# A state-space scan over 32 batches: where in TensorE's step the sum of a past state stands

## What is computed

```python
dA = jnp.exp(jnp.einsum('bld,dn->bldn', dt, A))          # 512 channels, 16 states
dB = jnp.einsum('bld,bln->bldn', dt, Bm)
def step(h, inp):
    dA_i, dB_i, u_i, C_i = inp
    h = dA_i * h + dB_i * u_i[:, :, None]
    y = jnp.einsum('bdn,bn->bd', h, C_i)
    return (h, y)
...
out = y * jax.nn.silu(z)
return out @ W_out.T
```

## Time and profile before

| | us |
|---|---|
| median of 2 runs | 3286.52 |
| lowest, highest | 3284.66, 3288.39 |
| the profiled execution, its time | 3282.21 |
| the profiled execution, its span | 3280.3 |
| granted TensorE clock, mean over the span | 0.967 |

### The profile page before, as it was taken

How to read it: one execution, slowest core, us unless ns; L and a number is a source line. 1 busy time by engine, 2 the same in 40 slices (tenths; PEclk the granted TensorE clock), 3 DMA queues, 4 the chain that set the end, 5 groups by cost and what they waited for, 6 DMA issues and landing times. The chain is left out here.

```text
span 3280.3 us, 54538 instructions
## 1 busy us (share of the span) xinstructions
PE 2964.9 (90%) x19138; PEld 2406.4 (73%) x19138; DVE 2839.4 (87%) x4799; ACT 2710.2 (83%) x5234; POOL 2229.4 (68%) x911
## 2 busy tenths in 40 slices
PE   6999999999999999999999999999999997566664
PEld 4777787777777777777787878787887877455453
DVE  4889999999999999999999999999999998544442
ACT  5999999999999999999999999999999996211110
POOL 1777676666766666666767676767767676377776
PEclk8999999999999999999999999999999999688888
DMA  3112211222222222211222222212222111477774
GB/s 112 59 59 69 70 59 61 68 71 70 71 70 62 65 70 71 71 61 60 69 70 71 71 70 70 71 61 70 71 70 71 61 56 33 129 148 148 149 150 78
DMA packets 196175, 252.98 MB, mean 77 GB/s; under 512 B 45664, under 2 KB 174144, under 8 KB 195904
## 3 DMA queue, kind: packets, MB, share of 16 engines
q1 hardware_dynamic: 171328, 211.73, 20.6%
q0 software_dynamic: 24576, 37.77, 7.0%
HBM read 188.36 MB, written 61.08 MB: 76 GB/s over the span
## 5 line engine op out<-in xcount | busy, mean ns | idle before, releaser
L354 POOL TENSOR_TENSOR hid<-hid,c_all 128x1536 f32<-128x1536 f32 x512 | 1770.1, 3461 | 873.9 <-DVEq L617 872.4
L622 DVE TENSOR_TENSOR_SCAN hid<-decay,hid,psB 128x1024 f32<-128x1024 f32 x512 | 1201.5, 2347 | 76.9 <-PE psB L942 27.6
L397 ACT ACTIVATE decay<-dt,a_neg 128x383 f32<-128x383 f32 x2048 | 1085.3, 604 | 0.0
L942 PE MATMUL psB<-ident,dbu_t 128*128 128x128 f32 x5760 | 806.0, 276 | 82.4 <-DVE hid L622 67.6
L385 ACT ACTIVATE dbu_t<-dtu_t,b_t 128x512 f32<-128x512 f32 x1312 | 853.2, 714 | 17.7 <-PE psB L942 16.6
L942 PEld LDWEIGHTS psB<-ident,dbu_t 128*128 128x128 f32 x5760 | 657.6, 142 | 245.3 <-issue 113.5
L954 PE MATMUL psY<-ident,hid 128*128 128x128 f32 x6144 | 758.0, 273 | 1.0 <-POOL hid L354 1.0
L954 PEld LDWEIGHTS psY<-ident,hid 128*128 128x128 f32 x6144 | 690.7, 142 | 1.6 <-POOL hid L354 1.3
L622 DVE TENSOR_TENSOR_SCAN hid<-decay,psB 128x512 f32<-128x512 f32 x512 | 623.0, 1217 | 10.3 <-PE psB L942 6.3
L1024 PE MATMUL psM<-u,w_dt 128*128 128x384 f32 x1024 | 349.1, 489 | 4.8 <-ACT u L427 3.3
L1422 ACT ACTIVATE e_sg<-e_psU 128x256 f32<-128x256 f32 x64 | 24.5, 383 | 340.3 <-PE e_psU L1464 225.4
(11 more groups left out here) (156 smaller groups left out, 3570.1 us busy)
## 6 DMA issues: line engine op xcount, KB each, us to landing
c_all<-bc_rows_dram SPq DMA_DIRECT2D x128, 768.0 KB, 4.9
out_dram<-h SPq DMA_DIRECT2D x64, 384.0 KB, 3.0
h<-out_dram SPq DMA_DIRECT2D x32, 384.0 KB, 3.6
x_weights_dram<-normed SPq DMA_DIRECT2D x32, 384.0 KB, 2.6
xt<-in_x_t_dram SPq DMA_DIRECT2D x32, 375.0 KB
xs<-in_x_dram SPq DMA_DIRECT2D x32, 256.0 KB
e_wg<-in_gate_dram SPq DMA_DIRECT2D x64, 128.0 KB
e_wu<-in_up_dram SPq DMA_DIRECT2D x64, 128.0 KB
```

Source lines behind the costliest of these rows:

```text
L354: nc.gpsimd.tensor_tensor(hid[k % 4][:, :, :], hid[k % 4][:, :, :], c_all[:, k, :].unsqueeze(1).to_broadcast([P, CH, L]), ALU.mult).then_i ...
L397: last = nc.scalar.activation(decay[k % 4][:, c, 1:L], dt[q][:, c, 1:L], ACT.Exp, scale=a_neg[:, c, k:k + 1])
L622: nc.vector.tensor_tensor_scan(h[:, lo:hi], flat(decay[k % 4])[:, lo:hi], flat(psB)[:, lo:hi], h[:, lo - 1:lo] if j else 0.0, ALU.mult, AL ...
L942: last = nc.tensor.transpose(flat(psB)[:, i * P:(i + 1) * P], dbu_t[k % 2][:, t, c * P:(c + 1) * P], ident[:, :])
```

## The change

In TensorE's loop the two calls of `sum_y` move from between the two groups of turns to behind the second. What stood between the groups otherwise (k=2 and k=5) stays there, and all that stood behind group 1 now stands behind group 1 and the sum. Nothing else is changed: no instruction, no wait, no buffer, no DMA, and no other engine's program.

```diff
@@ -1082,10 +1082,6 @@
                 for k in range(NS):
                     if scans:
                         turn_dbu(b, q, k, 0)
-                    if scans and k >= 3:
-                        sum_y(b, k - 3)
-                    if back and k < 3:
-                        sum_y(m, k + NS - 3)
                     if k == 2:
                         if front:
                             project_xin(n, 0)
@@ -1096,6 +1092,10 @@
                             route(c)
                     if scans:
                         turn_dbu(b, q, k, 1)
+                    if scans and k >= 3:
+                        sum_y(b, k - 3)
+                    if back and k < 3:
+                        sum_y(m, k + NS - 3)
                     if k == 0:
                         if front:
                             turn_normed1(n, 0)
```

## The result

The changed kernel takes 3495.49 us (median of 2 runs, 3493.82 to 3497.16) against 3286.52: a ratio of 1.064, 95% interval 1.062 to 1.066. It is 209 us slower, where 153 had been forecast; the time lies within the range, close to its upper end. The profiled execution took 3497.16 us with a span of 3495.3, to be set beside 3280.3.

A forecast was written before the change was run, and what follows sets the result against it. VectorE was taken to set the pace, with TensorE following closely. Terms 79.1 + 33.0 + 26.0 + 9.6 + 21.1 - 15.5 = 153 us, added to the kernel before, gave 3440 us, range 3395 to 3500.

The forecast's parts named there:

- the walk: One batch followed from the places where TensorE waited for VectorE: 153 us slower, own range 3410 to 3470, chance 0.60.
- rival 1: TensorE's clock falls at step 3 after new idle: 43 to 69 us more if in every batch, 3483 to 3509; chance 0.18.
- gate: At k=2 VectorE waits for TensorE's sum of state 15 before gating batch m's output: 2.55 us, 31 batches.
- row maximum: At k=5 VectorE waits for the scores, a 16.78 us TensorE path after step 3's idle: 1.10 us, 30 batches.
- short scan of step 8: VectorE's scan waits for TensorE, counted from step 5's long scan: 0.84 us in 31 batches.
- short scan of step 11: VectorE's scan waits for TensorE, counted from step 9's long scan: 0.32 us in 30 batches.
- out block and what leads to it: At k=15 VectorE waits to add the out block, counted from step 13's long scan: 0.68 us, 31 batches.
- given back at the long scans: VectorE's earlier waits for TensorE's turns vanish, as group 1 comes no later: 0.5 us a batch, 15.5 us.
- the two consequences: Sum no longer fills TensorE's wait before group 1, later work up to 1.31 us late; next group 0 1.31 us late.
- rival 2: ScalarE's lead over the scans is used up and its 1.3 us wait is paid too: up to 3480, chance 0.08.
- The time with only the gate paid: Only VectorE's wait at the gate is paid, the other four terms could vanish: 3350 us, chance 0.10.
- The case of no slowdown: VectorE's 0.5 us a batch is given back and nothing is paid: 3271 us, chance 0.04.

The follow-up runs named there:

- step 2 alone: Kernel before, with the sum moved behind both groups of turns in step 2 only: 3328.2 us, ratio 1.014.
- all but step 3: Changed kernel with the sum of step 3 put back between the groups: 3427.3 us, ratio 1.044.
- steps 8 and 15 alone: Kernel before, with the sum moved behind both groups in steps 8 and 15 only: 3273.1 us, ratio 0.9974.
- the filled step 3: Changed kernel with group 0's four turns in step 3 made four times in all batches but the first: 3467.8 us, ratio 1.057.
- The filled runs: Two runs: changed kernel with group 0's turns in step 3 made four times (3467.8 us) or twice (3478.6 us).

## Why the prediction was right, and where it fell short

The direction, the mechanism and the places were right. The number was 56 us too low: 3495 lies above the 3410 to 3470 that the walk had for its own range, and it is within the stated range because that one was drawn to hold rival 1. The clock of rival 1 makes 30 of the 56, the other 26 are terms that came out larger than forecast; that both together still fit under 3500 is luck.

Term by term, for a batch at the full clock (1537.51 to 1628.56), us a batch:

| term | forecast | measured shift |
|---|---|---|
| gate | 2.55 | 2.69 |
| score of the experts | 0 | 0.46 |
| row maximum | 1.10 | 1.28 |
| short scan of step 8 | 0.84 | 0.84 |
| short scan of step 11 | 0.32 | 0.32 |
| out block and what leads to it | 0.68 | 0.72 |
| given back at the long scans | -0.50 | -0.35 |
| sum | 4.99 | 5.96 |

Gate to gate it is 91.05 - 84.98 = 6.07; the remaining 0.11 are shifts under 0.06 each.

**The bound and the two consequences** were right. VectorE set the pace; each of its new waits was paid in full, and the waits stand at the five places named, ended by the releasers named. The run with step 2 alone bears it out: with one sum on its path the gate waits 1.31 us, with two 2.62. One wait that VectorE pays at the full clock, that of the score, had not been named.

**The missed term** is the score, 0.46 us, and it belongs to the sum for row maximum. The sum of 16.78 us counted TensorE's z projection of step 5 at its issue price, as if its buffer were free. It isn't:

```profile
1553.64 1.98 PE L1014 MATMUL psM<-w_in,turned 128*128 128x512 f32 x4 [0.41 <-ACT zs_t L422]
```

It fills the buffer that the first z projection filled, and ScalarE reads that out late, since it had itself waited 1.71 us for the last x_in projection, which came behind a sum:

```profile
1546.78 0.67 ACT L413 ACTIVATE u<-psM,b_cv,w_cv 128x384 f32<-128x384 f32 x1 [1.71 <-PE psM L1006]
```

The projection starts 1.01 us behind group 0 of its step (1552.63) instead of 0.44, and takes 1.83 us to the next instruction instead of 1.72, together 0.68 us. The whole path, from the tied turn at 1543.05 to the row maximum at 1560.48, is 17.43 us where 16.78 were forecast. These 0.65 us are all that the score and the row maximum have above their terms (1.74 against 1.10). I had named ScalarE's waits and called them hidden while its lead lasts; I looked at its decays only, not at the buffers it hands back to TensorE. This is rival 2 in a small form: 0.65 us of the 1.3. The run with all but step 3 agrees: with that sum back, ScalarE waits 0.41 us for the last x_in projection instead of 1.71, the z projection starts 0.70 us behind group 0, and the score has no wait. What another order of the buffers would save wasn't tried.

**The give-back** was taken whole at 0.50 us. Of it 0.31 come back at the long scans of steps 8 and 15 (0.35 in the sum above with one of 0.04 at step 12); the rest of the recorded 0.36 and 0.16 us is the 0.1 that stands between a short and a long scan anyway (1.32 us from start to start at a length of 1.22). The run with steps 8 and 15 alone gained 0.31 a batch, the same number.

**The clock.** Here the likeliest case, a full clock in every batch, was wrong, and rival 1 came true, if in 18 of 30 batches. Step 3 of the batch at the full clock, and of the next one:

```profile
1543.05 1.09 PE L942 MATMUL psB<-ident,dbu_t 128*128 128x128 f32 x8 [1.73 <-DVE hid L622]
1543.98 1.47 PE L954 MATMUL psY<-ident,hid 128*128 128x128 f32 x12
```

```profile
1631.74 0.63 PE L942 MATMUL psB<-ident,dbu_t 128*128 128x128 f32 x4 [0.63 <-DVE hid L622]
1634.10 1.52 PE L942 MATMUL psB<-ident,dbu_t 128*128 128x128 f32 x8 [1.73 <-DVE hid L622]
1635.41 2.76 PE L954 MATMUL psY<-ident,hid 128*128 128x128 f32 x12
```

The granted clock over 4 us from there (columns as in the earlier trace rows):

```profile
1543.00:1547.00 4.00, 3.95 (x25) 3.20 (x26) 3.90 (x4) 2.29 (x6) 2.81 (x2) 1.00 0.00 0
1634.00:1638.00 4.00, 3.90 (x21) 3.90 (x22) 3.90 (x5) 2.12 (x5) 2.80 (x2) 0.58 0.02 4
```

The idle of 0.63 and 1.73 us came as forecast (0.7 and 2.0). In the first batch the turns and the sum take 1.09 and 1.47 us, in the next 1.52 and 2.76, and the clock over the 4 us is 0.58, which is mostly the lower level, 1.2 GHz. Of the 30 batches with a gate up to 2828 us, 18 are slow so, 12 are not, with the same idle before them. A slow one takes 92.72 us gate to gate instead of 91.05. My price was 1.4 us, the measured one 1.67; VectorE waits it out in the convolution ahead of step 4 (the 13.6 us of L718) and before the score (1.0 us instead of 0.4). The forecast had taken the row with 1.46 us idle and not the one with 2.47, because 4 blocks of work stand between the two new stretches. That choice between two ends was the step that failed; the mechanism was on record as rival 1. 18 x 1.67 = 30 us, and the filled step 3 gave back 28.

**The account.** 153 us were forecast, 209 measured. The clock is 30 of the missing 56, the score and the row maximum (0.64 x 30) 19, the gate (0.14 x 31) 4, the give-back (0.15 x 31) 5. That is 58.

**The other rivals.** The time with only the gate paid, 3350, was not to be seen, since no path term vanished. Its nearest relative, step 2 alone, took 3328, for its gate pays one sum only. The case of no slowdown exists, with the sum behind in steps 8 and 15; it is bounded by what VectorE waited before.

## What to carry to other kernels

Work that stood in an engine's wait cost nothing here, and moved behind the wait it was charged to everything queued behind, also several steps on. So count from the last place where the engine waited to each instruction that the pacing engine wants, and compare it with that engine's own distance. Put the sum back, or leave it, where the engine waits for its partner, not where the partner waits for it; when something is moved, the places of waiting move too, and the count starts anew. Read-outs of shared buffers by a third engine belong in this count, and so does the clock of an engine that gets a new idle stretch in each round.

## What the chip showed that was not expected

The same idle stretch gave a full clock in 12 batches and a lower one in 18, without any difference in the work ahead of it that the trace shows. From the fourth batch on, each batch at the full clock is followed by one or two slow ones, never by three; what sets this rhythm no run shows. With 1.29 us in place of 1.73 it was 6 of 30, with 0.42 none, and so adding 12 turns without a use to each batch made the kernel 28 us faster.

The length of one stretch does not decide it alone. In step 6 of the same trace TensorE idles 1.48 us in 29 of the 30 batches, longer than the 1.29 above, and the clock over the 4 us from there is 1.00 each time:

```profile
1564.94 1.09 PE L942 MATMUL psB<-ident,dbu_t 128*128 128x128 f32 x8 [1.48 <-DVE hid L622]
```

What step 3 has besides is a stretch of 0.63 us just before, with only 4 blocks between the two. The filled runs changed two things at once, the length of the second stretch and the work between them, so which of the two counts is not shown.
